# q and k projected ahead of v, the edge counts moved beside v, in a fused graph and attention block

## The chip, the cores and the metric

The kernel runs on one core of one Trainium2 chip, as one program of five instruction streams: TensorE (PE), VectorE (DVE), ScalarE (ACT), GpSimd (POOL) and SyncE (SP, which here issues DMAs). The metric is the time of one execution on the device, in microseconds; less is better. The time before is the median of 3 runs, 1683.38 us (1680.94 to 1683.82).

## The reference, cut to what matters

N = 1250 nodes, D = 768 columns, 21250 edges (`src`, `dst`). A normalised x goes through three graph attention layers (4 heads of 192 columns) and, independently of them, through a linear attention with 12 heads of 64 columns and 256 random features; then a routed feed-forward with 8 experts.

```python
# graph: for each of 3 layers
h = (x1 @ W).reshape(N, 4, 192)
e = leaky_relu(as_n[src] + ad_n[dst])
p = exp(e - segment_max(e, dst)[dst]);  alpha = p / segment_sum(p, dst)[dst]
out = segment_sum(alpha * h[src], dst)
# attention
q, k, v = x @ w_qkv.T                      # 12 heads of 64
q_prime = exp(q @ proj.T - |q|^2/2 - max over features)    + eps
k_prime = exp(k @ proj.T - |k|^2/2 - max over everything)  + eps
context = k_prime^T v
out = q_prime @ context / (q_prime @ sum(k_prime))
```

The maximum for k runs over all heads, nodes and features, so no k feature can be computed before all of q and k is projected.

## The kernel before

The edges are not gathered. A dense matrix `count` of 1250 x 1250 (how many edges go from u to n) is built once, and each of the 12 graph heads (3 layers of 4) is then dense: `edge_max` finds each node's maximum over its neighbours, `edge_z`, `edge_exp` and `weigh` make the weights, `gather` multiplies them with h.

How `count` comes about: GpSimd scatters the edges with 170 indirect DMAs (L2173) into three tables in DRAM; `tab_in(t)` (SyncE, L2287) loads 128 rows of each of the three tables; `count(t)` adds them and the diagonal on VectorE (L1499 to L1503) and casts the sum on ScalarE (L1951); `count_turn(t)` turns it on TensorE (L1086); `absent(t)` writes from it a mask of the edges that don't exist (VectorE, L1512). t runs over 10 tiles of 128 nodes. `tab_in` waits for all scatters, and its buffers are two sets of three tiles. `edge_max` (VectorE, L1524) needs the whole mask; there are 120 of it, 10 for each head.

The projections: `v(i)`, 20 groups of 18 matmuls (a tile t and a half of 384 columns each; a product is three bf16 matmuls, high x high, high x low, low x high), copied by ScalarE (L1932) to `v_row` and stored by SyncE. `qk(m, part)`: 36 chunks, three (512, 512 and 226 nodes) for each of 12 pieces of 128 columns; the pieces are k of pair 0, q of pair 0, k of pair 1 and so on. `qk_split(m)` squares and copies a chunk on ScalarE (L1942, L1946) and takes the low parts on VectorE (L1452, L1455); `norms` sums the squares (L1034, L1465); `k_top` (L1048 on TensorE, L1475 on VectorE) finds the maximum of a piece's k products, five steps during the q piece that follows. Three PSUM banks go round between v and qk. The weights are loaded by `w_load(j)` (SyncE, L2237) into three `stage` tiles and split by `w_split(j)` in high (ScalarE, L1898) and low (VectorE, L1360). `pair_in(p)` loads k, v and q of a head pair back from DRAM; pair 0 has buffers of its own (`k_first`, `v_first`, `q_first`). After the last chunk come `top_max`, `top_turn` and `top_spread`, the maximum over everything, with `warm_mix` matmuls that compute nothing between them; then the six pairs: `dash` (features, L1122), `k_exp`, `k_sum`, `q_exp`, `q_turn`, `q_out`.

What sets the order: one list of steps, `ORDER`, made at build time by Python generators. Each engine's program walks it and emits the steps it has a function for, so each engine works in that order, and an engine that waits in one step holds back all its later ones. `paced` and `spread` weave two tracks: the first is `projection_steps` and then `mix_steps`; the second is `graph_steps`, which starts where the first has reached chunk `COUNTS_AT` and then adds `COUNT_RATE` count steps, or `EARLY_EDGE_RATE` edge steps, to each tick of the first. A tick is half a chunk of q and k, or one v group. In the order before, v comes first (20 ticks), then q and k (72), with `tab_in(0)` at chunk 17, `count(0)` one tick behind it, `count_turn` and `absent` of a tile two ticks behind its `count`; 12 `edge_max` stand ahead of `dash(0,k,0)`.

```python
COUNTS_AT = 17
COUNT_RATE, EARLY_EDGE_RATE, FIRST_EDGE_RATE, EDGE_RATE, ATTENTION_RATE = 0.5, 0.75, 1.1, (1.1, 0.5), (0.4, 0.5)
```

## Time and profile before

| | |
|---|---|
| median of 3 runs | 1683.38 us |
| the profiled execution | 1689.38 us |
| its span, first to last instruction | 1687.6 us |
| mean granted TensorE clock | 0.959 of full |
| TensorE busy | 1522.4 us (90%) |
| VectorE busy | 1178.1 us (70%) |
| ScalarE busy | 680.3 us (40%) |
| GpSimd busy | 431.6 us (26%) |
| chain that ended last | PE 46%, DVE 18%, POOL 17%, DMA 8%, issue 7%, ACT 4% |

The profile is one execution. Busy shares are means over stages with different limits, so the stages are read apart: normalisation, x1 and the layers' h up to 313.5 us, v to 376 us, q and k with the counts to 581 us, the attention's six pairs beside the graph heads, and so on. In a timeline a row is one or several like instructions with the idle time of the engine ahead of them and what ended it in brackets. The granted clock has two levels, 1.00 (2.4 GHz) and 0.50 (1.2 GHz); between them stand means of a window.

### The profile page before, as it was taken

Reading aid. Unit: us, or ns where it says so; the run is one execution under the profiler, and the core shown is the slowest. Engines: PE = TensorE matmul, PEld = TensorE weight load, DVE = VectorE, ACT = ScalarE, POOL = GpSimd, SP = SyncE. Lnnn points to the kernel's source line nnn. Section 1 sums busy time; section 2 is a strip of 40 time slices with the busy share of each in tenths; the row PEclk is TensorE's granted clock in tenths of the full one; section 3 lists DMA queues with packets and bytes.
Section 4 is the critical chain, followed back from the end, with each engine's and each line's share of the span. In section 5 each row is a group of like instructions: output and inputs, shape, how many; then the busy total and the mean of one; then the engine's idle time right before and its main releaser. Section 6 shows DMA issues by size and latency. Waiting matters only on the chain.

```text
span 1687.6 us, 26057 instructions
## 1 busy us (share of the span) xinstructions
PE 1522.4 (90%) x10179; PEld 1188.2 (70%) x10205; DVE 1178.1 (70%) x2645; ACT 680.3 (40%) x1359; POOL 431.6 (26%) x251
## 2 busy tenths in 40 slices
PE   3979999999868798989899989998999999995897
PEld 2556666555434467988888988888888986664786
DVE  6677674105567889999999587767866753787565
ACT  3421001013132267877687764435543531342110
POOL 3688888888600000000000000000000000000553
PEclk9989999999979899999999999999999999997899
DMA  9434545354653325233332244433432222661992
GB/s 350 91 67 105 122 85 124 62 90 89 138 192 125 111 67 146 61 110 89 95 91 77 66 126 156 161 126 128 137 122 74 80 71 73 241 244 58 341 303 73
DMA packets 196620, 213.72 MB, mean 127 GB/s; under 512 B 81551, under 2 KB 149789, under 8 KB 196498
## 3 DMA queue, kind: packets, MB, share of 16 engines
q1 hardware_dynamic: 119874, 187.01, 34.9%
q0 software_dynamic: 75760, 22.70, 8.5%
q10 hardware_dynamic: 864, 2.36, 0.4%
q8 instruction: 80, 1.31, 0.3%
q14 instruction: 42, 0.34, 0.1%
HBM read 144.74 MB, written 68.40 MB: 126 GB/s over the span
## 4 chain that ended last, share of the span: by engine, by line
PE 46%; DVE 18%; POOL 17%; DMA 8%; issue 7%; ACT 4%; SPq 0%; POOLq 0%; ACTq 0%; DVEq 0%
PE bank L1105 18%; POOL table L2173 17%; PE bank L931 5%; PE bank L932 5%; PE bank L933 5%; DVE junk L1524 4%; DMA table<-amount,place 4%; PE bank L1269 2%; PE bank L1165 2%; DVE eb L1559 2%; PE bank L1137 2%; PE bank L1122 2%; DVE eb L1568 2%; PE bank L1180 1%; DVE q_max L1591 1%
## 5 line engine op out<-in xcount | busy, mean ns | idle before, releaser
L1105 PE MATMUL bank<-hb,eb 128*128 128x193 f32 (+3 forms) x2400 | 418.8, 332 | 14.4 <-ACT node L1976 9.3
L1105 PEld LDWEIGHTS bank<-hb,eb 128*128 128x128 f32 (+3 forms) x2400 | 399.6, 191 | 20.6 <-issue 9.5
L2173 POOL DMA_INDIRECT table<-amount,place x170 | 347.8, 2046 | 72.7 <-issue 48.5
L2179 POOL IOTA iota8i<- 128x8 int32 x1 | 0.1, 135 | 944.0 <-DMA node_rows<-node 944.0
L1559 DVE SCALAR_TENSOR_TENSOR eb<-shift_b,as_low,shift_b 128x640 f32<-128x640 f32 (+1 forms) x240 | 196.4, 860 | 0.3 <-PE bank L1105 0.2
L1962 ACT ACTIVATE eb<-eb,asd 128x640 f32<-128x640 f32 (+1 forms) x240 | 181.5, 812 | 28.9 <-DVE eb L1559 28.9
L1568 DVE SCALAR_TENSOR_TENSOR eb<-eb,count 128x1280 f32<-128x1280 f32 (+1 forms) x120 | 174.5, 1454 | 2.5 <-ACT eb L1962 2.5
L1524 DVE CUSTOM_DVE_ANT_0 junk<-ab,absent 128x1250 bf16<-128x1250 f32 x120 | 174.3, 1453 | 1.5
L931 PE MATMUL bank<-w_o_hi,aT_hi 128*128 128x384 bf16 (+1 forms) x360 | 119.2, 331 | 0.0
L932 PE MATMUL bank<-w_o_lo,aT_hi 128*128 128x384 bf16 (+1 forms) x360 | 119.0, 330 | 0.0
L931 PE MATMUL bank<-wg_hi,x1T_hi 128*128 128x384 bf16 (+3 forms) x360 | 119.0, 330 | 0.0
L933 PE MATMUL bank<-w_o_hi,aT_lo 128*128 128x384 bf16 (+1 forms) x360 | 119.0, 330 | 0.0
L933 PE MATMUL bank<-wg_hi,x1T_lo 128*128 128x384 bf16 (+3 forms) x360 | 118.9, 330 | 0.0
L932 PE MATMUL bank<-wg_lo,x1T_hi 128*128 128x384 bf16 (+3 forms) x360 | 118.8, 330 | 0.0
L1398 DVE TENSOR_TENSOR h_row<-bank,bgr 128x384 f32<-128x384 f32 (+1 forms) x60 | 32.5, 555 | 64.9 <-PE bank L933 62.3
L932 PE MATMUL bank<-xnT_lo,wq_hi 128*128 128x512 bf16 (+1 forms) x212 | 73.5, 347 | 4.3 <-DVE wq_lo L1360 2.6
L933 PE MATMUL bank<-xnT_hi,wq_lo 128*128 128x512 bf16 (+1 forms) x215 | 74.2, 345 | 0.2
L1908 ACT ACTIVATE wg_hi<-stage 128x776 bf16<-128x776 f32 x18 | 15.3, 850 | 135.4 <-DVE stage L1374 106.5
L931 PE MATMUL bank<-xnT_hi,wq_hi 128*128 128x512 bf16 (+1 forms) x201 | 69.6, 346 | 0.1
L2001 ACT ACTIVATE ef<-bank,q_shift 128x256 f32<-128x256 f32 (+1 forms) x120 | 50.5, 473 | 46.9 <-DVE q_shift L1596 46.7
L2193 POOL DMA_INDIRECT sr<-xf_rows,from_row x16 | 23.6, 1477 | 173.8 <-DVE to_row L1798 156.4
L1976 ACT ACTIVATE node<-bank 128x386 f32<-128x386 f32 (+1 forms) x72 | 29.3, 442 | 88.4 <-PE bank L1105 88.4
(286 smaller groups left out, 3040.6 us busy)
## 6 DMA issues: line engine op xcount, KB each, us to landing
w<-in_w SPq DMA_DIRECT2D x16, 1152.0 KB, 10.9
shift_b<-shift_rows SPq DMA_DIRECT2D x24, 625.0 KB, 5.8
h_rows<-h_row SPq DMA_DIRECT2D x27, 388.0 KB
hb<-h_rows SPq DMA_DIRECT2D x12, 873.0 KB
ar<-node_rows SPq DMA_DIRECT2D x27, 384.0 KB
table<-zero POOLq DMA_DIRECT2D x3, 3054.0 KB, 20.1
tab<-table SPq DMA_DIRECT2D x27, 312.5 KB, 3.6
qk_rows<-qk_row SPq DMA_DIRECT2D x12, 625.0 KB
```

The source lines that it names most:

```text
L931: T.matmul(out_ap, lhs[0], rhs[0], start=first, stop=False, skip_group_check=skip)
L932: T.matmul(out_ap, lhs[0], rhs[1], start=False, stop=False, skip_group_check=skip)
L933: return T.matmul(out_ap, lhs[1], rhs[0], start=False, stop=last, skip_group_check=skip)
L1105: ins = T.matmul(bank[w // 2][0:M, c0:c0 + GC + 1], p[0:K, u, w * P:w * P + M], hv[0:K, t, 0:GC + 1], start=opens and u == 0 and w % 2 == ...
L1122: ins = T.matmul(bank[3 + g % 2][0:R, hh * FEATS:(hh + 1) * FEATS], parts[:, hh, at(t)], feats[f][:, :], start=hh == 0 and f == 0, stop=f ...
L1137: ins = T.matmul(cv[:, m, hh, :], ef[g % 4][0:R, hh, m * 128:(m + 1) * 128], values_of(pair)[0:R, t, hh, :], start=t == 0 and m == 0 and h ...
L1524: V.tensor_tensor_reduce(out=junk[0:R, :], in0=ab[lh % 2][0:R, :], in1=absent[0:R, t, :], scale=1.0, scalar=-BIG, op0=ALU.add, op1=ALU.max ...
L1559: ins = V.scalar_tensor_tensor(eb[i % EDGE_BUFFERS][:, u, 0:w], low, as_low[:, t, lh:lh + 1], high, ALU.add, ALU.max)
L1568: V.scalar_tensor_tensor(e, e, 1.0, count[:, 2 * pair:2 * pair + 2, ns], ALU.min, ALU.mult).then_inc(sem["edge_w"], 1)
L1962: ins = A.activation(e[:, u, 0:w], e[:, u, 0:w], ACT.Exp, bias=asd[:, t, 8 * l + hh:8 * l + hh + 1])
L2001: ins = A.activation(ef[g % 4][0:R, hh, :], bank[3 + g % 2][0:R, hh * FEATS:(hh + 1) * FEATS], ACT.Exp, bias=bias)
L2173: G.indirect_dma_start(tables[i], bass.IndirectOffsetOnAxis(place[:, c:c + 1], axis=0), amount16[:, c:c + 1], None, compute_op=ALU.add).th ...
```

## The change

- **Order.** q and k come first, right behind `as_rows` (the last step of the layers). v's 20 groups come last, behind the 36 chunks. The pieces' weights are numbers 24 to 35 now (`FIRST_QK`), v's 36 to 41 (`FIRST_V`); v's are loaded and split in the last chunks. v waits for the copies of the last q and k chunks at its start.
- **Counts.** `COUNTS_AT` is chunk 35, the last. The rate is one count step a tick. `count` stands two ticks behind its `tab_in` (one before), `count_turn` and `absent` two ticks behind `count` as before. `count_turn(0)` stands ahead of v(0) on TensorE, nine more between v(0) and v(9). Then 16 `edge_max` up to the last v group, at 1.6 a tick.
- **Top maximum.** `top_max`, `top_turn` and `top_spread` stand behind v(1), v(3) and v(5); their `warm_mix` matmuls (8, 4 and 6) are gone.
- **First pair.** ScalarE copies pair 0's part of v straight from PSUM to `v_first`, so an even v group has two copies (128 and 256 columns) and an odd one 384 columns as before. `v_out` stores only pairs 1 to 5; `pair_in(0)` loads only k and q and stands 20 ticks sooner. `first_ones` sets the column of ones in `v_first`.
- **Places in SBUF.** The table tiles, `count16`, `junk`, `k_first`, `q_first` and `v_first` lie elsewhere, so that v's weights can live beside them; `tab_in` also waits for the store of `as_rows`.

```diff
+FIRST_QK, FIRST_V = 24, 36
-COUNTS_AT = 17
-COUNT_RATE, EARLY_EDGE_RATE, FIRST_EDGE_RATE, EDGE_RATE, ATTENTION_RATE = 0.5, 0.75, 1.1, (1.1, 0.5), (0.4, 0.5)
+COUNTS_AT = 35
+COUNT_RATE, EARLY_EDGE_RATE, FIRST_EDGE_RATE, EDGE_RATE, ATTENTION_RATE = 1, 1.6, 1.1, (1.1, 0.5), (0.4, 0.5)
...
 def projection_steps(done):
     yield "feats_in", 0
-    for t in range(NT):
-        for half in range(2):
-            yield "v", 2 * t + half
-            yield None
-        if t >= NT - 2:
-            yield "w_load", 30 + t - NT + 2
-    yield "w_split", 30
...
+            k = m - NC * 2 * PAIRS + KD + 1
+            if part == 0 and 0 <= k <= KD:
+                if k < KD:
+                    yield "w_load", FIRST_V + k
+                if k:
+                    yield "w_split", FIRST_V + k - 1
...
-    yield "top_max", 0
-    yield "warm_mix", 8
...
+    for i in range(2 * NT):
+        yield "v", i
+        if i in (1, 3, 5):
+            yield ("top_max", "top_turn", "top_spread")[i // 2], 0
+        yield None
     done.add("projected")
...
-    yield from paced((in_step([(3, lambda t: [("count_turn", t), ("absent", t)]), (1, lambda t: [("count", t)]),
+    yield from paced((in_step([(4, lambda t: [("count_turn", t), ("absent", t)]), (2, lambda t: [("count", t)]),
                                (0, lambda t: [("tab_in", t)])], NT), COUNT_RATE))
...
+                values = bank[(NC * 2 * PAIRS + i) % 3][0:R, 0:HROWS].rearrange("p (a h c) -> p a h c", h=2, c=HD)
+                if half == 0:
+                    A.activation(v_first[0:R, t, :, 0:HD], values[:, 0, :, :], ACT.Copy)
+                    ps, values = ps_rest, values[:, 1:, :, :]
+                A.activation(v_out[t % 2][0:R, ps, :, 0:HD], values, ACT.Copy).then_inc(sem["v_copy"], 1)
...
+                sy.wait_ge("as_rows_out", 16)
```

**SyncE, around the first table loads.** Before: `stage` is a q or k piece's weights, `qk_rows` the store of a piece, `tab` the tables; brackets name the semaphores waited for.

```order
L2237 DMA stage_170<-in_wT_qkv 128x6x128 [waits w_lo]
L2277 DMA qk_rows<-qk_row_193 128x2500 [waits qk_lo]
L2295 DMA ab_248<-as_rows 128x1250 [waits as_rows_out]
L2287 DMA tab_143<-table 128x1250 [waits scatter1,scatter0,scatter2,h_out2,h_mm]
L2287 DMA tab_144<-table 128x1250
L2287 DMA tab_230<-table 128x1250
L2237 DMA stage_171<-in_wT_qkv 128x6x128 [waits w_lo]
L2287 DMA tab_145<-table 128x1250
L2287 DMA tab_146<-table 128x1250
L2287 DMA tab_147<-table 128x1250
L2277 DMA qk_rows<-qk_row_194 128x2500 [waits qk_lo]
L2287 DMA tab_143<-table 128x1250 [waits counted]
```

After: the six rows of 128x768 are v's weights.

```order
L2293 DMA qk_rows<-qk_row_189 128x2500 [waits qk_lo]
L2253 DMA stage_165<-in_wT_qkv 128x768 [waits w_lo]
L2253 DMA stage_166<-in_wT_qkv 128x768 [waits w_lo]
L2253 DMA stage_167<-in_wT_qkv 128x768 [waits w_lo]
L2293 DMA qk_rows<-qk_row_190 128x2500 [waits qk_lo]
L2253 DMA stage_165<-in_wT_qkv 128x768 [waits w_lo]
L2253 DMA stage_166<-in_wT_qkv 128x768 [waits w_lo]
L2253 DMA stage_167<-in_wT_qkv 128x768 [waits w_lo]
L2293 DMA qk_rows<-qk_row_189 128x2500 [waits qk_lo]
L2312 DMA ab_244<-as_rows 128x1250 [waits as_rows_out]
L2304 DMA tab_103<-table 128x1250 [waits scatter1,scatter0,scatter2,h_out2,h_mm]
L2304 DMA tab_104<-table 128x1250
```

The table loads moved behind every weight load, and two whole sets (six rows) stand ahead of anything that needs them; before, a weight load and a store of q stood behind the wait for the scatters.

**VectorE, around the first count.** Before: `kmax` is `k_top`, `sq` and `qk_row` are `qk_split`, `wq_lo` a weight's low part, `diag` is `norms`.

```order
L1475 TENSOR_REDUCE kmax<-bank 98x1
L1452 TENSOR_TENSOR sq_190<-sq_190 128x226
L1455 SCALAR_TENSOR_TENSOR qk_row_194<-bank,qk_row_194 128x226
L1360 TENSOR_TENSOR wq_lo<-stage_170,wq_hi 128x768
L1465 TENSOR_SCALAR diag<-bank 128x4x2
L1499 TENSOR_TENSOR count<-tab_143,tab_144 128x1250
L1501 TENSOR_TENSOR count<-count,tab_230 128x1250
L1503 TENSOR_TENSOR count<-count,ident 128x128
L1452 TENSOR_TENSOR sq_188<-sq_188 128x512
L1455 SCALAR_TENSOR_TENSOR qk_row_193<-bank,qk_row_193 128x512
L1465 TENSOR_SCALAR diag<-bank 128x4x2
L1499 TENSOR_TENSOR count<-tab_145,tab_146 128x1250
```

After:

```order
L1462 TENSOR_TENSOR sq_186<-sq_186 128x226
L1465 SCALAR_TENSOR_TENSOR qk_row_190<-bank,qk_row_190 128x226
L1513 TENSOR_TENSOR count<-tab_103,tab_104 128x1250
L1515 TENSOR_TENSOR count<-count,tab_248 128x1250
L1517 TENSOR_TENSOR count<-count,ident 128x128
L1475 TENSOR_SCALAR diag<-bank 128x4x2
L1513 TENSOR_TENSOR count<-tab_249,tab_250 128x1250
L1515 TENSOR_TENSOR count<-count,tab_251 128x1250
L1517 TENSOR_TENSOR count<-count,ident 128x128
L1475 TENSOR_SCALAR diag<-bank 128x2
L1475 TENSOR_SCALAR diag<-bank 98x2
L1526 TENSOR_SCALAR absent<-bank 128x8x128
```

The first `count` moved from between chunks 17 and 18 to behind the last chunk; what follows it is the next counts and masks, no longer q and k.

**TensorE, at the last chunk before the first count_turn.** Before, inside piece 6 (`wq`, 226 nodes), a chunk's second part ends and the next chunk begins:

```order
L933 MATMUL bank<-xnT_hi,wq_lo 128x226
L931 MATMUL bank<-xnT_hi,wq_hi 128x226
L932 MATMUL bank<-xnT_lo,wq_hi 128x226
L933 MATMUL bank<-xnT_hi,wq_lo 128x226
L1086 MATMUL bank<-ident_61,count_0_148 128x128 x9
L1086 MATMUL bank<-ident_61,count_0_148 98x128
L931 MATMUL bank<-xnT_hi,wq_hi 128x512
L932 MATMUL bank<-xnT_lo,wq_hi 128x512
```

After, the end of q and k and the start of v:

```order
L1040 MATMUL bank<-halves,sq_184 128x2 x8
L1040 MATMUL bank<-halves,sq_185 128x2 x8
L1040 MATMUL bank<-halves,sq_186 128x2 x2
L1040 MATMUL bank<-halves,sq_186 98x2 x2
L1092 MATMUL bank<-ident_61,count_0_148 128x128 x9
L1092 MATMUL bank<-ident_61,count_0_148 98x128
L937 MATMUL bank<-wv_hi,xnT_hi 128x384
L938 MATMUL bank<-wv_lo,xnT_hi 128x384
L939 MATMUL bank<-wv_hi,xnT_lo 128x384
```

`count_turn(0)` (L1086 before, L1092 after) now has nothing of q and k behind it: v(0) is the next work of TensorE.

## Rows read from the trace of the kernel before

**Rows 1.** Busy time by stretch: PE, PEld, DVE, ACT, POOL, then PEclk, DMA share, GB/s

```profile
313.50:376.00 62.50, 59.96 (x361) 36.67 (x362) 2.37 (x11) 11.00 (x22) 54.27 (x28) 0.98 0.48 73
376.00:458.00 82.00, 78.67 (x640) 43.78 (x649) 45.37 (x82) 21.80 (x43) 66.47 (x32) 1.00 0.55 108
458.00:470.00 12.00, 2.91 (x22) 1.87 (x22) 3.88 (x7) 2.22 (x3) 0.00 (x0) 0.70 0.90 293
470.00:536.00 66.00, 49.73 (x396) 29.11 (x401) 45.70 (x93) 21.81 (x32) 0.00 (x0) 0.85 0.46 152
536.00:581.00 45.00, 36.71 (x303) 20.32 (x304) 38.02 (x79) 6.90 (x15) 0.00 (x0) 0.89 0.20 72
627.00:922.00 295.00, 269.57 (x1942) 254.81 (x1941) 275.94 (x454) 214.52 (x477) 0.00 (x0) 0.96 0.34 94
```

**Rows 2.** Timeline of TensorE: start us, us, instruction, idle before and what ended it

```profile
313.54 0.53 PE L931 MATMUL bank<-wv_hi,xnT_hi 128*128 128x384 bf16 x1
...
376.08 0.38 PE L932 MATMUL bank<-xnT_lo,wq_hi 128*128 128x512 bf16 x1 [2.62 <-DVE wq_lo L1360]
...
469.55 0.36 PE L1034 MATMUL bank<-halves,sq 128*128 128x2 bf16 x4 [9.04 <-DVE diag L1465]
...
489.84 0.73 PE L1086 MATMUL bank<-ident,count 128*128 128x128 bf16 x10
...
580.74 0.27 PE L1122 MATMUL bank<-feats_hi,k_first 128*128 128x256 bf16 x1
```

**Rows 3.** Timeline of ScalarE: chunks 5 and 17, first and last cast

```profile
399.52 0.36 ACT L1942 ACTIVATE sq<-bank 128x226 f32<-128x226 f32 x1 [2.95 <-PE bank L933]
...
450.18 0.36 ACT L1942 ACTIVATE sq<-bank 128x226 f32<-128x226 f32 x1 [2.95 <-PE bank L933]
...
466.27 1.25 ACT L1951 ACTIVATE count<-count 128x1250 bf16<-128x1250 uint16 x1 [14.75 <-DVE count L1503]
...
529.77 1.25 ACT L1951 ACTIVATE count<-count 128x1250 bf16<-128x1250 uint16 x1 [5.29 <-DVE count L1503]
```

**Rows 4.** Timeline of VectorE around the first counts

```profile
452.91 0.39 DVE L1455 SCALAR_TENSOR_TENSOR qk_row<-bank,qk_row 128x226 bf16<-128x226 f32 x1
...
464.25 0.81 DVE L1499 TENSOR_TENSOR count<-tab,tab 128x1250 uint16<-128x1250 uint16 x1 [10.01 <-DMA tab<-table]
...
465.94 0.29 DVE L1503 TENSOR_TENSOR count<-count,ident 128x128 uint16<-128x128 uint16 x1
...
474.44 0.94 DVE L1512 TENSOR_SCALAR absent<-bank 128x1024 bf16<-128x1024 bf16 x3
```

**Rows 5.** SyncE: first table load in the timeline; landing of all 30

```profile
457.85 1.27 SPq L2287 DMA_DIRECT2D tab<-table  x3
...
DMA to landing us min/median/max: 2.8/3.6/5.5
```

**Rows 6.** Groups by form: v matmuls, v copies, scatters from 314, 376 and 426 us

```profile
L931 PE MATMUL bank<-wv_hi,xnT_hi 128*128 128x384 bf16 x108 | 35.8, 332 | 0.0
...
L1932 ACT ACTIVATE v_row<-bank 128x384 f32<-128x384 f32 x18 | 8.9, 492 | 41.3 <-PE bank L933 38.9 <-issue 2.4
...
L2173 POOL DMA_INDIRECT table<-amount,place x27 | 53.8, 1994 | 8.2 <-issue 7.9 <-DMA table<-amount,place 0.3
...
L2173 POOL DMA_INDIRECT table<-amount,place x22 | 45.6, 2073 | 7.4 <-issue 6.4 <-DMA table<-amount,place 1.0
...
L2173 POOL DMA_INDIRECT table<-amount,place x11 | 24.0, 2181 | 6.8 <-DMA table<-amount,place 4.3 <-issue 2.4
```

**Rows 7.** VectorE's edge_max: group from 581 to 922 us; last start

```profile
L1524 DVE CUSTOM_DVE_ANT_0 junk<-ab,absent 128x1250 bf16<-128x1250 f32 x98 | 142.4, 1453 | 1.4
...
L1524 DVE DVE_READ_ACCUMULATOR2_ANT m_col<- x23: 80/83/85, 845.6 to 922.5; 128x1 f32 x20, 98x1 f32 x3
```

**Rows 8.** Two windows of 4 us behind the pause, columns as in Rows 1

```profile
464.00:468.00 4.00, 0.00 (x0) 0.00 (x0) 1.91 (x3) 1.73 (x3) 0.00 (x0) 0.50 1.00 367
...
472.00:476.00 4.00, 3.92 (x28) 2.14 (x27) 2.91 (x8) 1.54 (x3) 0.00 (x0) 0.86 0.87 279
```

More of the change, by code:

```diff
@@ L656, in program @@
         absent = put("absent", [P, NT, N], BF16)
+        at_att1 = cursor[0]
         att1 = put("att1", [P, NT, 128])
+        assert cursor[0] <= r_b
+        cursor[0] = at_att1
+        tab = [[put(f"tab0{j}", [P, N], U16) for j in range(2)], []]
         assert cursor[0] <= r_b
@@ L695, in program @@
         wv = [put(f"wv_{p}", [128, KD, D], BF16) for p in ("hi", "lo")]
-        after_v = cursor[0]
-        tab = [[put(f"tab{i}{j}", [P, N], U16) for j in range(2 + i)] for i in range(2)]
-        count16 = [put(f"count16_{i}", [P, N], BF16) for i in range(2)]
-        assert cursor[0] <= r_d
-        cursor[0] = r_c
         k_first, q_first = put("k_first", [128, 2, N], BF16), put("q_first", [128, 2, N], BF16)
         v_first = put("v_first", [P, NT, 2, HD + 1])
-        assert cursor[0] <= after_v
+        after_first = cursor[0]
+        count16 = [put("count16_0", [P, N], BF16)]
+        assert cursor[0] <= r_d
         cursor[0] = r_c
@@ L771, in program @@
         cursor[0] = r_f - size([P, N], U16)
-        tab[0].append(put("tab02", [P, N], U16))
+        count16.append(put("count16_1", [P, N], BF16))
         cursor[0] = r_e
@@ L798, in program @@
         assert cursor[0] <= 229368
+        cursor[0] -= 2 * size([P, N], F32)
+        tab[0].append(put("tab02", [P, N], U16))
+        tab[1] += [put(f"tab1{j}", [P, N], U16) for j in range(2)]
+        assert cursor[0] <= after
+        cursor[0] = r_f
+        tab[1].append(put("tab12", [P, N], U16))
         cursor[0] = r_f
@@ L1006, in v @@
                 for k in range(KD):
-                    pe.wait_ge("w_lo", 24 + k + 1)
-                    ins = three(bank[i % 3][0:R, 0:HROWS], [u[:, k, at(t)] for u in xnT], [w[:, k, cs] for w in wv],
+                    pe.wait_ge("w_lo", FIRST_V + k + 1)
+                    ins = three(bank[r % 3][0:R, 0:HROWS], [u[:, k, at(t)] for u in xnT], [w[:, k, cs] for w in wv],
                                 k == 0, k == KD - 1)
@@ L1477, in k_top, with first_ones @@
                 ins.then_inc(sem["k_max"], 1)
+            def first_ones(_):
+                ve.wait_ge("h_mm", 2 * NT * LAYERS)
+                V.memset(v_first[:, :, :, HD:HD + 1], 1.0).then_inc(sem["v_set"], 1)
             def top_max(_):
@@ L1844, in vector_program @@
                         w_part=w_part, x1=x1, h=h, as_rows=as_rows_, same=same_, place=place_, feats_in=feats_in, qk_split=qk_split, norms=norms,
-                        k_top=k_top, top_max=top_max, top_turn=top_turn, top_spread=top_spread, count=count_, absent=absent_, edge_max=edge_max, shifts=shifts, weigh=weigh,
+                        k_top=k_top, first_ones=first_ones, top_max=top_max, top_turn=top_turn, top_spread=top_spread, count=count_, absent=absent_, edge_max=edge_max, shifts=shifts, weigh=weigh,
                         finish=finish, q_exp=q_exp, divide=divide, out_split=out_split,
@@ L2332, in finish, with values_in @@
                     S.dma_start(rest, node[half][0:LAST, whole, 0:GC]).then_inc(sem[f"node_out{half}"], 16)
+            def values_in(pair):
+                for j in range(2):
+                    sy.wait_ge(f"v_out{j}", 16 * HALF)
+                full, rest = by_tiles(v_rows[pair], 0, NT)
+                vv = values_of(pair)[:, :, :, :].rearrange("p t h c -> p t (h c)")
+                S.dma_start(vv[:, 0:FULL, :], full).then_inc(sem[f"v_in{pair % 2}"], 16)
+                S.dma_start(vv[0:LAST, FULL, :], rest).then_inc(sem[f"v_in{pair % 2}"], 16)
             def pair_in(pair):
                 i = pair % 2
[L2336 removed]
+                if pair:
+                    sy.wait_ge("qk_mm", NC * 2 * PAIRS)
                     sy.wait_ge("v_mm", 2 * NT)
[L2338 to L2339 removed]
                 for j in range(2):
                     sy.wait_ge(f"qk_out{j}", 16 * (PAIRS if pair else 1))
[L2342 removed]
                 if pair >= 2:
```

93 lines of the change are left out of this document (42 added, 51 removed), and 2 rows, old and new, of the table TAKEN_OVER.

## The prediction

> **What bounds the kernel now.** I read the table of windows first [rows 1], then the timelines of TensorE, ScalarE and VectorE around the projections [rows 2 to 4], and the SyncE and GpSimd rows last. Up to 458 us TensorE is busy 96% of the time (60.0 of 62.5 us, 78.7 of 82): first the 20 groups of v, then q and k. From 458 to 581 us it is busy 2.9 of 12, 49.7 of 66 and 36.7 of 45 us, so some 34 us are idle there, and its mean clock is 0.70, 0.85 and 0.89, so more is lost below full speed [rows 1]. Two things make this hole. First, `count` stands in the middle of q and k: VectorE sits idle for 10.0 us until the first tables land, ScalarE 14.75 us behind it, and TensorE, which cannot reuse its three banks without their copies, 9.0 us [rows 2 to 4]. Second, the ten `count` steps run one by one through VectorE, ScalarE (63.5 us from the first to the last, 7.1 us each) and back, with q and k pieces queued behind each [rows 3]. The scatters that fill the tables end just before 457.85 us, when SyncE issues the first load [rows 5]: they are why nothing of `count` can start sooner. From 627 us until the last `edge_max` at 922 us VectorE is busy 94% and TensorE 91% [rows 1, 7].
>
> So from 313.5 to 581 us the end is set by TensorE's work plus its holes, and what is saved there moves everything behind it, since from `dash(0,k,0)` on the order is the same, four `edge_max` apart.
>
> **q and k first.** They start at 313.5 us, where v started, instead of 376.1: 62.5 us earlier [rows 2]. Their pace without `count` is seen in before: ScalarE takes chunk 5 at 399.52 and chunk 17 at 450.18 us, two rounds of six chunks (five `k_top` each), 25.3 us a round [rows 3]. The first six end at 399.5 - 62.5 = 337.0, plus 1.0 for the start below full clock that v has now (v's first matmul reads 0.53 us where 0.33 is the mean [rows 2, 6]); five more rounds are 126.7 us: chunk 35 reaches ScalarE at 464.7 us. The weights of pieces 24 and 25 are loaded during the last layer and wait for nothing late; before, their absence cost 2.62 us ahead of the first chunk [rows 2], which the 62.5 us hold.
>
> **v's weights** are now loaded and split in the last twelve chunk steps. Six ScalarE copies go beside matmuls (ScalarE is busy 22 of 82 us there [rows 1]). The six VectorE subtractions go on an engine 55% busy; the last may push `count(0)` by 1.0 us. Were loads late, ScalarE would wait with the squares behind it, but three banks cover about two steps; I take 0 of 0 to 3 us.
>
> **The scatters.** They run under it all and must end early enough. After the last one the first load takes 6.4 us until VectorE can add (457.85 to 464.25 [rows 4, 5]). VectorE itself is free 3.1 us after chunk 35 reaches ScalarE (chunk 17: 450.18 to 453.30 [rows 3, 4]) plus the 1.0 above, at 468.8. So the scatters have 4.5 us of slack. They could end sooner (`pair_in(0)` moves with less to load, and the 11 scatters from 426 us, beside it now, took 2181 ns against 1994 [rows 6]) or later (more stores of q and k under them). I take no delay, and 0 to 6 us for the range.
>
> The Trainium skill (SBUF — State Buffer, section "SBUF: two separate sides") says that GpSimd is locked out and cannot write its DMA descriptors while VectorE runs an operation in a two-port mode, which speaks against moving VectorE's work under the scatters. Were it true of all its operations here, the time would be the 1671 us of the third rival.
>
> **From the last q and k chunk to v.** `count(0)` is three adds, 2.0 us from 464.25 to 466.23 [rows 4]; the cast on ScalarE is 1.25 us [rows 3]; so the first `count_turn`, which stands ahead of v(0) on TensorE, starts at 468.8 + 2.0 + 1.25 = 472 us. TensorE idles from 464.7 to there but for the norms, some 7 us, where v(0) could have run: this is what the change leaves lying. Behind the 9.04 us pause of before the clock stood at 0.50, then 0.86 in the next four-us windows [rows 2, 8]; I add 2.4 us for some 5 us at the lower level.
>
> **v beside the counts.** A v group costs 59.9 / 20 less the slow start, 2.94 us [rows 2]; a `count_turn` 0.73 us [rows 2]. So TensorE needs 3.67 us in each step that has both. VectorE needs 1.95 + about 1.1 (`absent`, 0.94 for its three pieces and gaps [rows 4]) = 3.1 us. ScalarE needs 1.25 + 0.49, and 0.16 more in even steps, where one copy of 384 becomes 128 and 256 columns (226 columns take 0.36 us and 384 take 0.49: 0.16 us of each copy do not shrink with it [rows 3, 6]). Keeping v in SBUF thus costs 1.6 us of ScalarE in all, hidden, and spares the load of `v_first`, hidden too. The table loads: each buffer set is used every second step, and its loop is issue and landing of three loads (1.3 + 3.6 us [rows 5]) + 1.95 = 6.9 us against two steps, 7.3 us. That is tight; the v stores share the queue. I add 1.5 us (0 to 17). Sum: 10 x 0.73 + 9 x 2.94 + 2.4 = 36.2, so the last `count_turn` ends at 508.2; 11 more groups, 32.3 us, in which VectorE does 16 `edge_max` (1.45 + 0.08 each, 24.5 us, hidden); with the 1.5 us 542.0 us. The top maximum and its turns go between v groups, so the 18 warming matmuls and the waits ahead of `dash` are gone. `dash(0,k,0)`, 580.7 us before [rows 2], comes at 542: **38.7 us** earlier.
>
> **Behind it.** 16 `edge_max` instead of 12 are done by then, 4 x 1.53 = 6.1 us less for VectorE in a stretch where it is the fuller engine. TensorE is 91% busy there, so at least 0 and at most 6.1 us come through; I take 1.8, since VectorE too waits for TensorE there.
>
> **The sum.** 38.7 + 1.8 = 40.5 us. The profiled execution took 1689.4 us (span 1687.6) and would take 1648.9; the median of the runs is 6.0 us below it, 1683.4, and becomes **1642.9 us**. The best case (no slow start or clock loss, no contention, weights free, all 6.1 us through: 1.0 + 2.4 + 1.5 + 1.0 + 4.3) is 1632.7.
>
> **Rivals.** (1) *The count steps stay dear.* They now cost 7.1 us each; the loop of tables, adds, cast and turn is the same, and ScalarE's v copy waits behind a cast that waits for VectorE. Nine steps at 7.1 instead of 3.67 give +31 us, 1674; at 5.5 us +16.5, 1659. Against it: the 7.1 us hold a whole chunk of q and k with its squares and `k_top`, now one v group, and a table load is issued two steps ahead of its adds, not one. (2) *The scatters end later*, by 8 us past their slack: 1651. In the busiest stretch, 426 to 458 us, 11 scatters at 2.3 us (1994 ns and 0.3 of issue [rows 6]) would fill 25.3 of 32 us: 6.7 were lost. (3) *VectorE holds up GpSimd.* VectorE was 0.55 busy from 376 to 458 us, with 0.04 before [rows 1]. If each busy microsecond stopped the scatters, the 59 us now filled would delay them 32 us, less the slack 28 us: 1671. The rows say 1994 ns a scatter with VectorE idle and 2073 beside it [rows 6]: 27 x 0.08 = 2 us, inside the slack. The rows decide against most of it. (4) *Slower than before: TensorE's clock stays at the lower level through v.* Its steps have pauses, and each v group at the lower level costs 2.94 us more. It decides from 40.5 / 2.94 = 14 of the 20 groups on; with all 20 the time is 1642.9 + 58.8 - 2.4 = 1699. Against it: after 9 us of pause the clock was back within some 5 us of dense matmuls [rows 8], and v's steps are dense. (5) *The tables are not early*: the first two sets are still tied to the last scatter. This is in the sum; only the later eight sets gain.
>
> **How the numbers follow.** Forecast, 1636 to 1652: 0.62. Better than 1636: 0.11. Rival 1 in full or half: 0.15. Rival 2 beyond 1652: 0.05. Rival 3: 0.03. Rival 4: 0.04 with its weaker forms, of which 0.03 slower than before. The range for 8 in 10 is 1631 to 1662. A measurement of this kernel tells about 0.2% (3.4 us) from no change: faster by more 0.94, within 0.02, slower 0.04.
>
> **What would show it.** Right: the first wq matmul near 313.5 us; ScalarE's last square near 465; the first table load at 452 to 462; one TensorE pause of 6 to 8 us, then v steps of 3.7 and 2.9 us; `dash(0,k,0)` near 542; the last `edge_max` 39 to 46 us sooner. Wrong: v steps over 5 us with VectorE waiting for `tab` (rival 1), GpSimd rows well over 2.1 us (3), a clock of 0.5 to 0.8 across v (4), a last scatter behind 462 us (2), or an end that moves by less than `dash(0,k,0)` does, which would mean that the stretch behind takes the gain back.

## The result, and the profile after

The changed kernel takes **1647.24 us** (median of 4 runs, 1643.71 to 1651.98) beside 1683.60 us for the kernel before (4 runs): a ratio of 0.9778, 95% interval 0.9761 to 0.9796. Forecast was 1642.9, with 1631 to 1662 as the range. Together with the later jobs there are 14 runs of the changed kernel, median 1648.1, and 46 of the kernel before, median 1686.5; the means lie 38.8 us apart (± 1.5; here and below ± is two standard errors of the difference of two means). The sum of the prediction was 40.5.

The profiled execution took 1647.98 us (span 1646.2), 41.4 us less than that of before. Its page; the two tables read as those of before do:

```profile
span 1646.2 us, 26056 instructions
...
PE 1506.8 (92%) x10187; PEld 1179.8 (72%) x10187; DVE 1180.3 (72%) x2646; ACT 680.2 (41%) x1369; POOL 434.3 (26%) x251
...
PE 49%; POOL 17%; DVE 14%; DMA 9%; issue 6%; ACT 4%; SPq 1%; POOLq 0%; ACTq 0%; DVEq 0%
```

TensorE's busy time fell by 16 us (1522.4 before): the 18 warming matmuls are gone and fewer matmuls ran at the low clock. The rest of the gain is idle time that is gone. Busy time by stretch, in the order of [rows 1] (PE, PEld, DVE, ACT, POOL, then PEclk, DMA share, GB/s):

```profile
470.00:510.00 40.00, 35.98 (x274) 23.08 (x275) 26.28 (x65) 16.28 (x24) 0.00 (x0) 0.93 0.75 235
510.00:545.00 35.00, 33.53 (x207) 20.84 (x205) 34.00 (x57) 7.38 (x19) 0.00 (x0) 1.00 0.40 97
545.00:590.00 45.00, 38.92 (x281) 30.56 (x282) 33.78 (x63) 31.67 (x73) 0.00 (x0) 0.94 0.46 123
590.00:881.00 291.00, 265.82 (x1911) 251.16 (x1910) 270.08 (x452) 211.31 (x469) 0.00 (x0) 0.96 0.34 95
```

Where [rows 1] had 16 us idle of 66 and a clock of 0.85 in the stretch of the counts, there are now 4 of 40 at 0.93. TensorE's timeline answers to [rows 2]:

```profile
312.87 0.63 PE L938 MATMUL bank<-xnT_lo,wq_hi 128*128 128x512 bf16 x1
...
465.39 0.28 PE L1054 MATMUL bank<-feats_hi,qk_row 64*128 64x256 bf16 x2 [1.26 <-DVE kmax L1485]
...
467.77 0.34 PE L1040 MATMUL bank<-halves,sq 128*128 128x2 bf16 x8 [1.27 <-DVE diag L1475]
470.34 0.36 PE L1040 MATMUL bank<-halves,sq 128*128 128x2 bf16 x4 [2.23 <-DVE diag L1475]
471.54 1.22 PE L1092 MATMUL bank<-ident,count 128*128 128x128 bf16 x10 [0.84 <-ACT count L1967]
472.56 0.53 PE L937 MATMUL bank<-wv_hi,xnT_hi 128*128 128x384 bf16 x1
...
542.65 0.27 PE L1128 MATMUL bank<-feats_hi,k_first 128*128 128x256 bf16 x1
```

The pause of 9 us in the middle of q and k has become one of four pieces (1.26, 1.27, 2.23 and 0.84 us) behind their end, and the step ahead of the pairs, `dash(0,k,0)`, comes at 542.65 instead of 580.74. ScalarE at the last chunk and at the first and last cast, as in [rows 3]:

```profile
464.17 0.36 ACT L1958 ACTIVATE sq<-bank 128x226 f32<-128x226 f32 x1 [2.22 <-PE bank L939]
...
470.15 1.25 ACT L1967 ACTIVATE count<-count 128x1250 bf16<-128x1250 uint16 x1 [5.37 <-DVE count L1517]
...
506.77 1.25 ACT L1967 ACTIVATE count<-count 128x1250 bf16<-128x1250 uint16 x1 [1.04 <-DVE count L1517]
```

From the first to the last of the ten casts it is 36.6 us, 4.07 us a step where it was 7.1. (In the two later profiled executions, `again` and `again2`, it is 37.4 and 35.4.) What the steps still wait for stands on VectorE, the first add of `count` (compare [rows 4]):

```profile
468.15 0.80 DVE L1513 TENSOR_TENSOR count<-tab,tab 128x1250 uint16<-128x1250 uint16 x1
471.08 0.81 DVE L1513 TENSOR_TENSOR count<-tab,tab 128x1250 uint16<-128x1250 uint16 x1 [0.88 <-DMA tab<-table]
476.24 0.81 DVE L1513 TENSOR_TENSOR count<-tab,tab 128x1250 uint16<-128x1250 uint16 x1 [2.18 <-DMA tab<-table]
481.38 0.81 DVE L1513 TENSOR_TENSOR count<-tab,tab 128x1250 uint16<-128x1250 uint16 x1 [2.29 <-DMA tab<-table]
484.26 0.80 DVE L1513 TENSOR_TENSOR count<-tab,tab 128x1250 uint16<-128x1250 uint16 x1
...
502.03 0.81 DVE L1513 TENSOR_TENSOR count<-tab,tab 128x1250 uint16<-128x1250 uint16 x1 [2.77 <-DMA tab<-table]
```

`count(0)` waits for nothing; six of the other nine wait for their tables, 11.3 us in all. SyncE's first table load, the landing of the 30, and the scatters (compare [rows 5, 6]; the second group is GpSimd's from 314 to 461 us, the first row its last scatter):

```profile
459.51 1.99 POOL L2189 DMA_INDIRECT table<-amount,place  x1 [0.30 <-DMA table<-amount,place]
...
463.37 8.05 SPq L2304 DMA_DIRECT2D tab<-table  x9
...
DMA to landing us min/median/max: 2.8/4.2/6.1
...
L2189 POOL DMA_INDIRECT table<-amount,place x59 | 123.9, 2101 | 23.8 <-issue 16.2 <-DMA table<-amount,place 7.7
```

A table takes 4.2 us to land (the median; 4.5 and 4.0 in `again` and `again2`), 3.6 before. The last `edge_max` behind the counts (the same group as [rows 7]) ends at 874.8 us, 47.7 sooner:

```profile
L1538 DVE DVE_READ_ACCUMULATOR2_ANT m_col<- x85: 81/83/87, 582.9 to 874.8; 128x1 f32 x76, 98x1 f32 x9
```

### The profile page after: what moved, and what is told of

It is laid out like the page before. It is cut to its first block, busy times and chain, and to the rows that moved or that the text cites. A ratio compares the mean times of both kernels' runs of the same rounds, so it can differ in the third digit from the quotient of the medians.

```text
span 1646.2 us, 26056 instructions
## 1 busy us (share of the span) xinstructions
PE 1506.8 (92%) x10187; PEld 1179.8 (72%) x10187; DVE 1180.3 (72%) x2646; ACT 680.2 (41%) x1369; POOL 434.3 (26%) x251
## 4 chain that ended last, share of the span: by engine, by line
PE 49%; POOL 17%; DVE 14%; DMA 9%; issue 6%; ACT 4%; SPq 1%; POOLq 0%; ACTq 0%; DVEq 0%
PE bank L1111 19%; POOL table L2189 17%; PE bank L937 6%; PE bank L939 6%; PE bank L938 6%; DMA table<-amount,place 4%; DVE junk L1538 3%; PE bank L1279 3%; PE bank L1147 2%; PE bank L1175 2%; PE bank L1128 2%; DVE eb L1573 2%; DVE eb L1582 1%; DMA tab<-table 1%; PE bank L1190 1%
## 5 line engine op out<-in xcount | busy, mean ns | idle before, releaser
L1111 PEld LDWEIGHTS bank<-hb,eb 128*128 128x128 f32 (+3 forms) x2400 | 398.7, 191 | 20.0 <-issue 10.6
L937 PE MATMUL bank<-xnT_hi,wq_hi 128*128 128x512 bf16 (+1 forms) x216 | 74.0, 343 | 0.0
## 6 DMA issues: line engine op xcount, KB each, us to landing
w<-in_w SPq DMA_DIRECT2D x16, 1152.0 KB, 11.3
```

Of the source, the lines that this page charges most:

```text
L937: T.matmul(out_ap, lhs[0], rhs[0], start=first, stop=False, skip_group_check=skip)
L1111: ins = T.matmul(bank[w // 2][0:M, c0:c0 + GC + 1], p[0:K, u, w * P:w * P + M], hv[0:K, t, 0:GC + 1], start=opens and u == 0 and w % 2 == ...
```

## The experiments

Each variant has 5 runs, but `late` 10, `early` 12 and `warm` 6. They were timed in three jobs: `late`, `lag1`, `vload` and `v2` in the first, `few`, `e12`, `v2again` and `again` in the second, `early`, `two`, `warm` and `again2` in the third. The changed kernel itself had 1649.00 us (5 runs, `again`) in the second and 1647.67 (5 runs, `again2`) in the third; the first had none, so its variants are set beside all 14 runs. The kernel before was in all three (1687.6, 1685.4 and 1687.5). Ratios are to the kernel before of the same job. Where one side has only 5 runs, the factor for 95% is nearer 2.3 to 2.8 standard errors than two, so differences that barely exceed their ± are weak.

The edits are shown shortened: `...` stands for what is left out, and inside `in_step` the steps are given by name instead of as lambdas.

### What each part is worth

**`late`**: the kernel before with its counts behind q and k, and v still first.

```diff
-COUNTS_AT = 17
-COUNT_RATE, EARLY_EDGE_RATE, ... = 0.5, 0.75, ...
+COUNTS_AT = 35
+COUNT_RATE, EARLY_EDGE_RATE, ... = 1, 1.6, ...
+    for _ in range(12):
+        yield None
     yield "top_max", 0
...
-    in_step([(3, count_turn, absent), (1, count), (0, tab_in)])
+    in_step([(4, count_turn, absent), (2, count), (0, tab_in)])
```

> The kernel before with v still first, but with the counts behind the last q and k chunk as in the changed kernel (rate 1, the same distances) and nothing of v beside them; 7 edge_max ahead of dash(0,k,0) instead of 12. It parts 'counts out of q and k' from 'v beside the counts'. Theory, that the gain is v's 58 us laid over the count chain: q and k end near 527 us without a hole, then TensorE stands almost idle for some 40 us of counts, dash(0,k,0) comes at 572 to 580 us against 580.7 before, and five edge_max more are left, 7.7 us of VectorE: 1678 to 1692, about the time before. Rival, that the interleaving of counts with q and k was the cost: dash(0,k,0) at 545 to 555 and 1650 to 1662.

Measured: 1681.51 us (10 runs), ratio 0.9964 [0.9948, 0.9980]. The time is as the theory said, and far from the rival's 1650 to 1662. The counts move behind q and k and take 3.9 us a step, but nothing runs under them. TensorE, while the counts run, then the warming matmuls behind the last `count_turn`, and `dash(0,k,0)`:

```profile
536.00:578.00 42.00, 18.24 (x106) 11.44 (x107) 33.07 (x68) 9.97 (x8) 0.00 (x0) 0.55 0.51 168
...
566.82 3.61 PE L1068 MATMUL bank<-ident 128*128 128x512 bf16 x8
...
577.69 0.27 PE L1124 MATMUL bank<-feats_hi,k_first 128*128 128x256 bf16 x1
```

It is busy 18 of 42 us at nearly the low clock, 0.55. The holes have been moved, not filled: 6 of the 39 us come from taking the counts out of q and k, and the other 33 from moving v's 20 groups behind q and k, with the direct copy of pair 0 that this needs (`vload`, below). Those 33 us hold two things that no run parts. v fills the stretch of the counts, and it also fills the wait for the top maximum: in `late` the top maximum and its warming matmuls take 10.9 us from 566.82 to `dash(0,k,0)`, in the kernel before 7.6 us (573.10 to 580.74), and in the changed kernel they stand between v groups. By these rows some 8 to 11 us of the 33 are the top maximum's, an estimate, and the rest the counts'.

**`early`**: the kernel before with the tables loaded two steps early, and nothing else.

```diff
-COUNT_RATE, EARLY_EDGE_RATE, ... = 0.5, 0.75, ...
+COUNT_RATE, EARLY_EDGE_RATE, ... = 0.5, 0.9, ...
-    in_step([(3, count_turn, absent), (1, count), (0, tab_in)])
+    in_step([(4, count_turn, absent), (2, count), (0, tab_in)])
```

> The kernel before with one part of the change alone: count two steps behind its table loads (one before) and count_turn two behind that; the early edge rate is 0.9 instead of 0.75, so that 12 edge_max still stand ahead of dash(0,k,0). The counts stay in the middle of q and k, v stays first. Theory A (early loads only help where the loads are what a step waits for; here a count step costs 7.1 us because a chunk of q and k lies in it, and the first tables still wait for the last scatter): -6 to +2 us against before. Rival B (the early loads make most of the gain): -15 us or more, count steps of 5 us instead of 7.1.

Measured: 1689.01 us (12 runs), ratio 1.0011 [0.9997, 1.0026]. No gain. In the order before, no count but the first waited for tables at all, so there was nothing for an early load to take away. The kernel before, its second and third `count` on VectorE, with no idle time ahead of them:

```profile
469.32 0.80 DVE L1499 TENSOR_TENSOR count<-tab,tab 128x1250 uint16<-128x1250 uint16 x1
...
475.30 0.80 DVE L1499 TENSOR_TENSOR count<-tab,tab 128x1250 uint16<-128x1250 uint16 x1
```

**`lag1`**: the changed kernel with `count` one step behind its loads again.

```diff
-    in_step([(4, count_turn, absent), (2, count), (0, tab_in)])
+    in_step([(3, count_turn, absent), (1, count), (0, tab_in)])
```

> The changed kernel with count one step behind its table loads instead of two (count_turn and absent three steps behind, as before the change). Theory: the loads are gated by free buffers, not by their place in the order, so the count chain ends where it does in the changed kernel (its last cast at 507 us); but two count_turn stand ahead of v(0) instead of one, so the pause of TensorE behind q and k grows from 7 to 10 or 11 us and one more v group is left behind the counts: dash(0,k,0) 2 to 4 us later (544 to 546), the time 1 to 4 us above the changed kernel's 1647 us. Rival, that the early issue itself is what hides the loads: each of eight adds waits some 3.6 us longer, 15 to 29 us more, 1662 to 1676.

Measured: 1655.86 us (5 runs, 1648.62 to 1660.69), ratio 0.9830 [0.9808, 0.9853], against 0.9778 and 0.9786 for the changed kernel: some 8 us (± 4.6, and ± 6 with the wider factor for 5 runs) lost. That lies between the two expectations, and the theory fell: the last cast comes at 510.29 and not at 507. Casts are 4.68 us apart, and VectorE waits longer for tables, here ahead of the ninth `count`:

```profile
505.16 0.81 DVE L1513 TENSOR_TENSOR count<-tab,tab 128x1250 uint16<-128x1250 uint16 x1 [5.68 <-DMA tab<-table]
...
548.70 0.27 PE L1128 MATMUL bank<-feats_hi,k_first 128*128 128x256 bf16 x1
```

`dash(0,k,0)` comes 6.0 us later than in the changed kernel (4.3 and 7.7 us later than in `again` and `again2`). The profiled execution was the shortest of the five, so its span (1646.9) tells little; the place of `dash` and the other four runs (1655 to 1661) agree. Two things are in this loss, the longer waits for tables and the second `count_turn` ahead of v(0), which the expectation names; v(0) starts at 474.64 instead of 472.56, so 2.1 us of the 6.0 are there before v begins. The same edit is worth nothing in the old order and some 8 us in the new one.

**`vload`**: the changed kernel with pair 0's v stored and loaded back.

```diff
-                if half == 0:
-                    A.activation(v_first[0:R, t, :, 0:HD], values[:, 0, :, :], ACT.Copy)
-                    ps, values = ps_rest, values[:, 1:, :, :]
...
-                    S.dma_start(v_rows[1:PAIRS, ...], v_out[t % 2][0:R, 1:PAIRS, ...])
+                    S.dma_start(v_rows[...], v_out[t % 2][...])
...
+        if i == 2 * NT - 1:
+            yield "values_in", 0
```

`values_in(0)` loads `v_first` from DRAM, behind the last store of v.

> The changed kernel without its third part: pair 0's v goes to v_row and to DRAM like the other pairs' and is loaded into v_first behind the last v store. Theory, from the sum that called this part hidden: in the old order it was hidden, in the new one it is not, since store and load of the last tile stand between v(19) and the first k_sum: some 4 us for the store to land and 5 for the load, so TensorE waits 4 to 8 us at k_sum(0,0), while VectorE goes on with edge_max. The time is 2 to 7 us above the changed kernel's 1647. Rival, that it stays hidden, because the first pair is held by VectorE and ScalarE anyway: 0 to 1.5 us.

Measured: 1653.59 us (5 runs), ratio 0.9800 [0.9771, 0.9829]; 5.4 us (± 4.1, and ± 5.3 with the wider factor for 5 runs) over the 14 runs of the changed kernel. `dash(0,k,0)` is where it was (542.53), and then `k_sum(0)` waits:

```profile
545.47 0.38 SPq L2349 DMA_DIRECT2D v_first<-v_rows  x1
...
549.66 1.97 PE L1143 MATMUL bank<-v_first,ef 128*128 128x65 f32 x8 [5.66 <-DMA v_first<-v_rows]
```

With v last, the way through DRAM (the last store at 542.1, the load from 545.5) ends behind the moment when pair 0 needs it: `k_sum(0)` starts 7.1 us behind `dash(0,k,0)`, and 3.7 us behind it in all three executions of the changed kernel, where the profile shows no data that its 2.2 us of idle time waits for. That is 3.5 us in the trace. Keeping v in SBUF pays for that.

### What still lies on the path

**`few`**: the last five scatters left out, and with them their edges in `count`.

```diff
-                for c in range(q * CP, min((q + 1) * CP, CHUNKS)):
+                for c in range(q * CP, min((q + 1) * CP, CHUNKS - 5)):
...
-                    sy.wait_ge(f"scatter{i}", 16 * added(CHUNKS, i))
+                    sy.wait_ge(f"scatter{i}", 16 * added(CHUNKS - 5, i))
```

> The changed kernel without its last 5 scatters, so the last 5 x 125 edges are left out of the table (the time is that of a kernel that scatters 165 of 170 chunks); everything else in its order. In the changed kernel the last scatter was issued at 459.51 us, the first table load at 463.37, count(0) at 468.15. Here the last scatter should be issued near 448.5 and the first table load near 452.5 us. Theory A (the scatters' late end sets only the last hundredths: VectorE is busy with the last q and k chunk until about 468 anyway, and only the table loads of the first three sets come sooner): count(0) stays within 1 us of 468, the first three count steps no longer wait for tables, the span is 0.5 to 3 us shorter. Rival B (the scatters bind: the 5.5 us by which their end moved are paid in full): count(0) near 463, dash(0,k,0) near 537, 5 us or more shorter.

Measured: 1645.88 us, ratio 0.9768 [0.9749, 0.9787]; the changed kernel beside it 0.9786 [0.9773, 0.9800]. The difference of the means is 2.4 us ± 3.3, so none is shown. The first table load:

```profile
452.82 3.88 SPq L2304 DMA_DIRECT2D tab<-table  x6
...
470.07 1.25 ACT L1967 ACTIVATE count<-count 128x1250 bf16<-128x1250 uint16 x1 [5.38 <-DVE count L1517]
```

It comes 10.5 us sooner than in the changed kernel, and the first cast at the same time (470.15 there). In these two executions the scatters had slack. It is not so in every one: in `again2` the first load came at 461.54 and `count(0)` waited 1.33 us for its tables.

**`e12`**: 12 `edge_max` ahead of `dash(0,k,0)` instead of 16.

```diff
-COUNT_RATE, EARLY_EDGE_RATE, ... = 1, 1.6, ...
+COUNT_RATE, EARLY_EDGE_RATE, ... = 1, 1.25, ...
```

> The changed kernel with 12 edge_max ahead of dash(0,k,0) instead of 16 (early edge rate 1.25 instead of 1.6), nothing else. It tests the term behind dash, 1.8 us taken of 0 to 6.1: if VectorE's four edge_max (1.53 us each) are on the path behind dash, the time rises by 6.1 us; if TensorE alone sets the pace there, by 0. From the profiled gain behind dash in the changed kernel (3.4 us) I expect +2 to +5 us, with dash(0,k,0) at 542.6 as before and the whole rise behind it.

Measured: 1646.41 us, ratio 0.9770 [0.9751, 0.9788]: no slower than the changed kernel (-1.8 us ± 3.5). The expected 2 to 5 us were a miss. The first row is the first `count`; the second is the last `edge_max`, 10.6 us later than the 874.77 of the changed kernel, and the end of the kernel does not follow it:

```profile
471.22 0.81 DVE L1513 TENSOR_TENSOR count<-tab,tab 128x1250 uint16<-128x1250 uint16 x1 [4.33 <-DMA tab<-table]
...
885.35 0.08 DVE L1538 DVE_READ_ACCUMULATOR2_ANT m_col<- 98x1 f32 x1
```

From `dash(0,k,0)` to the end it took 1105.7 us here, and 1103.6, 1104.2 and 1106.9 in the three profiled executions of the changed kernel. The first row shows the other side of `few`: the last scatter was issued at 461.56 here, though the edit does not touch the scatters, the first load at 465.45, and then `count(0)` did wait, 4.33 us.

**`two`**: two of three table loads, so that the third table's edges are missing from `count`.

```diff
-                for j in range(TABLES):
+                for j in range(TABLES - 1):
...
-  V.tensor_tensor(count[:, t, :], count[:, t, :], tb[2][:, :], ALU.add)
+  V.tensor_tensor(count[:, t, :], count[:, t, :], tb[1][:, :], ALU.add)
```

> The changed kernel with the third table's load left out; the second add of count reads the second table again, so the edges of the third table are left out and the work of every engine is as it was, with 640 KB instead of 960 KB a count step. In the changed kernel a step from cast to cast takes 4.07 us, where TensorE's work is 3.67. Theory A (the table loads set the step: DMA share 0.9 to 1.05 in the waits): casts 3.7 us apart or less, no wait of VectorE for tables over 0.5 us from the third step on, dash(0,k,0) 3 to 4 us sooner, the time 2 to 5 us less than the changed kernel's. Rival B (the chain of add, cast and turn sets it): still 4.0 us a step, same time.

Measured: 1646.70 us, ratio 0.9761 [0.9738, 0.9785], beside 0.9759 of the changed kernel. The casts, first and last, and the landing of the 20 loads:

```profile
471.50 1.25 ACT L1967 ACTIVATE count<-count 128x1250 bf16<-128x1250 uint16 x1 [5.38 <-DVE count L1517]
...
503.19 1.25 ACT L1967 ACTIVATE count<-count 128x1250 bf16<-128x1250 uint16 x1 [1.76 <-DVE count L1517]
...
DMA to landing us min/median/max: 2.7/3.5/4.6
```

That is 3.52 us a step instead of 4.07, and one wait of VectorE (1.0 us) in place of six: the table loads do set the part of the step above TensorE's own 3.67. From the first v matmul to `dash(0,k,0)` it takes 66.6 us (473.91 to 540.47), and 70.1, 72.5 and 68.9 in the three executions of the changed kernel. But v started 1.4 us later here than in the first of them, and the time as a whole moves by no more than can be measured (-0.5 ± 2.3 us). So the loads cost 2 to 6 us within that stretch; how much of it reaches the end stays open.

The Trainium skill (DMA: Bandwidth & Descriptors, section "Anatomy of one DMA — SWDGE (gpsimd) path") gives, for one DMA on another kind of queue, 2.0 us and the bytes over 436 GB/s. By it, if all bytes in flight are counted as one DMA, three tables of 320 KB are an estimated 4.2 us and two 3.5. The traces agree loosely at best: the medians are 4.2, 4.5 and 4.0 in the three executions of the changed kernel and 3.5 here, but 3.6 in the kernel before, which also loads three at a time, and the worst of thirty is 6.1 to 7.0 in the changed kernel.

**`v2`** and **`v2again`**: `v(0)` and `v(1)` ahead of `count_turn(0)`, the count track two ticks later, run in two jobs.

```diff
-COUNT_RATE, EARLY_EDGE_RATE, ... = 1, 1.6, ...
+COUNT_RATE, EARLY_EDGE_RATE, ... = 1, 2.0, ...
...
-        if m == COUNTS_AT:
-            done.add("scattered")
...
     def last_split(m):
         if m == NC * 2 * PAIRS - 1:
+            done.add("scattered")
             yield "qk_split", m
```

> The changed kernel with the whole count track two steps later in the order, so that v(0) and v(1) stand ahead of count_turn(0) on TensorE; the edge rate is 2.0 so that again 16 edge_max stand ahead of dash(0,k,0). Theory: the pause of 7 us behind q and k (464.5 to 472 us) is TensorE's to lose; two v groups, 5.9 us, fill it and the clock does not fall (1 to 2 us more), while the count chain on VectorE, ScalarE and the DMA queues starts where it did. dash(0,k,0) at 535 to 539 instead of 542, the time 2 to 6 us below the changed kernel, 1641 to 1645. Rival, that the count chain with its table loads and the 16 edge_max behind it set the end of this stage: dash(0,k,0) stays at 541 to 543 and the time within 1.5 us of the changed kernel's.

> The same kernel as v2 (v(0) and v(1) ahead of count_turn(0), the count track two ticks later, 16 edge_max ahead of dash), beside the changed kernel on the same chip, to tell whether it is faster than the changed kernel. Theory A (the pause of some 7 us ahead of v(0) is on the path, and v2 gives back part of it): 2 to 4 us less than the changed kernel's own time in this job, ratio to before 0.001 to 0.0025 lower. Rival B (the pause is made up for elsewhere): no difference.

Measured: 1645.50 us, ratio 0.9761 [0.9738, 0.9783], and 1645.72 us, ratio 0.9759 [0.9734, 0.9784]; beside the changed kernel in one job 5.0 us (± 3.8) less, over both jobs (10 runs against 14) 2.8 us (± 2.5) less. With the wider factors this is ± 5.1 and ± 2.6: the gain is likely, at the edge of what can be told. In `v2again`:

```profile
468.25 0.44 PE L936 MATMUL bank<-wv_hi,xnT_hi 128*128 128x384 bf16 x1
...
538.79 0.27 PE L1127 MATMUL bank<-feats_hi,k_first 128*128 128x256 bf16 x1
```

v starts 4.3 us sooner and `dash(0,k,0)` comes 3.9 sooner. In `v2` they lie at 467.09 and 538.84. So the pause that the change leaves is on the path as far as `dash(0,k,0)`, and v can fill some 4 of its 7 us.

**`warm`**: 22 matmuls that compute nothing in the pause, placed ahead of these steps (the second number is how many).

```diff
 k_top(29):        +  keep_warm(6, 5)
 norms(34):        +  keep_warm(6, 5)
 norms(35):        +  keep_warm(6, 9)
 count_turn(0):    +  keep_warm(6, 3)
```

> The changed kernel with 22 matmuls that compute nothing (into a free bank, 512 columns, 0.21 us each) in the four waits of TensorE between the last q and k chunk and v(0): 5 ahead of the last k_top, 5 and 9 ahead of the last two norms, 3 ahead of count_turn(0); nothing waits for them. In the changed kernel the clock was 0.61 and 0.54 from 468 to 476 us, count_turn(0) took 1.22 us and the first 10 matmuls of v(0) came 0.32 us apart instead of 0.16. Theory A (the low clock costs about 2 us: 1.6 in v(0), 0.5 in count_turn(0)): clock 1.00 through the stretch, 1 to 2.5 us less. Rival B (nothing, since the count steps behind wait for tables anyway): first v matmuls at 0.33 us but casts and dash(0,k,0) where they were.

Measured: 1647.04 us, ratio 0.9773 [0.9745, 0.9801] (6 runs), beside 0.9759 of the changed kernel in this job. The windows of four us at the pause, the changed kernel's first, then those of `warm`:

```profile
468.00:472.00 4.00, 0.93 (x14) 0.81 (x11) 3.02 (x7) 1.25 (x1) 0.00 (x0) 0.61 0.74 257
472.00:476.00 4.00, 4.00 (x20) 2.23 (x18) 2.02 (x7) 1.25 (x1) 0.00 (x0) 0.54 1.02 342
```

```profile
468.00:472.00 4.00, 1.62 (x11) 0.47 (x8) 2.11 (x5) 1.24 (x1) 0.00 (x0) 1.00 0.62 220
472.00:476.00 4.00, 3.94 (x36) 2.78 (x37) 2.79 (x8) 1.26 (x2) 0.00 (x0) 1.00 0.98 325
...
472.63 0.33 PE L937 MATMUL bank<-wv_hi,xnT_hi 128*128 128x384 bf16 x1
...
541.64 0.27 PE L1132 MATMUL bank<-feats_hi,k_first 128*128 128x256 bf16 x1
```

The granted clock stays at its higher level, and v's first matmul takes 0.33 us instead of 0.53. `dash(0,k,0)` lies within the 541.0 to 544.4 us of the changed kernel's three executions, and the time shows no gain. With ± 4.6 us between the two means, the 2 us of this term can't be shown or excluded.

**`again`** and **`again2`**: the changed kernel itself.

> The changed kernel itself, timed again beside its variants: ratio to the kernel before 0.976 to 0.980. Its median and its profiled execution show how far the two lie apart: the prediction took 6.0 us, its first result had 0.7.

> The changed kernel itself once more, beside the two variants of it in this job: ratio to before 0.976 to 0.980.

Measured: 1649.00 us, ratio 0.9786 [0.9773, 0.9800], and 1647.67 us, ratio 0.9759 [0.9736, 0.9782]. Three profiled executions of one program put `dash(0,k,0)` at 542.65, 544.44 and 541.04 us. Differences of up to 3.4 us between two profiles say nothing here.

## Why the prediction was right, point by point

- **q and k first: right.** Forecast: q and k from 313.5, chunk 35 at ScalarE at 464.7. The trace: 312.4 and 464.17. The 25.3 us a round of before held (chunk 5 at 337.49, chunk 29 at 438.84, four rounds of 25.34) without v's weights showing (0 taken of 0 to 3 us).
- **The scatters: right in cost, wrong in detail.** The first load was put at 457.85 with 4.5 us of slack. It came at 463.37, 5.5 us later, and `count(0)` still started at 468.15 without a wait, forecast 468.8. `few` shows that loads 10 us sooner bring nothing measurable. Loads at 460.60 (`lag1`), 461.54 (`again2`) and 465.45 (`e12`) cost `count(0)` 1.48, 1.33 and 4.33 us, where 463.37 cost nothing: the slack ends somewhere between 460 and 463 us, with the execution, since both the landing and VectorE's own readiness move. The last scatter isn't where it is by the order alone: in the changed kernel's three executions it was issued at 459.51, 455.08 and 457.71.
- **The pause: right.** `count_turn(0)` at 472, forecast, was 471.54; v(0) at 472.56. It took the clock loss as 2.4 us; the rows give 0.5 in `count_turn(0)` and 1.6 in v(0) (ten matmuls 0.32 instead of 0.16 us apart). Its reading of [rows 8] is loose: the window at 0.50 lies inside the pause, and the one behind it, 468 to 472 us, was at 0.50 as well. `v2` confirms that this is what the change leaves lying.
- **v beside the counts: right, with one term somewhat small.** From the first `count_turn` to the last the forecast has nine steps of 3.67 us, 1.5 for contention and 2.4 for the clock, 36.9 us. The trace has 37.3 (471.54 to 508.84), and 39.7 and 36.1 in `again` and `again2`. Since the clock took 2.1 of it, contention was 2.2 us where 1.5 was put (4.6 and 1.0 in the other two, if the clock cost the same there). `two` names the cause: the tables, with 33.8 us for the same nine steps. The estimate of their loop, 6.9 us for two steps, went by the landing of 3.6 us; with 4.2 us it is 7.5, more than the 7.3 of two steps. From v's start to `dash(0,k,0)` the forecast has 69.3 us (472.7 to 542.0); the profile has 70.1.
- **`dash(0,k,0)`: forecast 542.0, measured 542.65.** That it came within 0.7 us is in part luck: two more executions of the same program lie at 544.44 and 541.04, and the 580.74 that the 38.7 us start from is one execution too.
- **"Keeping v in SBUF ... spares the load of v_first, hidden too": wrong.** That holds for the order before, where v ended at 376 us, 205 us ahead of `dash(0,k,0)`. In the new order the load costs some 5 us (`vload`: 5.4 in the means, 3.5 in the trace). It cost the sum nothing, since the sum had no term for a load that the change doesn't make, but the reason was wrong: it is a part without which the rest would be worth some 5 us less.
- **"Behind it", 1.8 of 0 to 6.1 us: not borne out.** The four `edge_max` are worth nothing measurable (`e12`), which fits TensorE, busy 265.8 of 291 us, setting the pace there; no run shows that by itself. The profile's 3.3 us (`dash` to the end 1106.9 before, 1103.6 after) is the spread of single executions: in the variants of the changed order other than `vload` (1110.2, with its wait) the same distance lies between 1098.2 (`lag1`) and 1107.4 (`few`), and in `early` it is 1102.7. Also the test "the last `edge_max` 39 to 46 us sooner" was wrong: it came 47.7 sooner, 10.6 later in `e12`, and the end heeds neither.
- **The level: off by 4 us.** The step that was off is "the median of the runs is 6.0 us below it". The kernel before's profiled execution (1689.4) was 2.9 us above the median of its 46 runs (1686.5), and three runs had put the median at 1683.4. The changed kernel's profile stood 0.7 above its first median. 1689.4 - 2.9 - 40.5 would have been 1646.0; against 14 runs with a median of 1648.1 the remaining 2 us are about the size of the term behind `dash`, and of the spread between executions. The first 4 runs alone give 1647.24, 4.3 above the forecast, within its range.
- **The rivals.** (1) Count steps of 7.1 or 5.5 us: no, 4.07. (2) The scatters 8 us past their slack: no; `count(0)` waited 0 to 1.3 us in the changed kernel's three executions. (3) VectorE holding up GpSimd: the 59 scatters from 314 to 461 us took 2101 ns on the mean with VectorE busy 87 of 147 us. Above the 1994 ns beside an idle VectorE [rows 6] that is 59 x 0.107 = 6 us. Part of it was there before too: the 60 scatters of [rows 6] took 123.4 us, 2057 ns on the mean, so what the new order adds is 59 x 0.044 = 2.6 us. It does not come near 32 us. (4) The clock was 1.00 from 476 us on. (5) Only the later tables came early, as put in the sum.
